# Inverse of the chunk matrix from 16x16 diagonal blocks, substituted from the last column on, with one link of 64x64 products

## The reference

```python
h = layernorm(x) * (1 + ca) + sa
x = x + ga * attn(h)
h = layernorm(x) * (1 + cb) + sb
x = x + gb * ffn(h)          # silu(w1 h) * (w2 h), gelu(h1 .), gelu(h2 .), w3 .
```

```python
A0 = -where(strict, einsum('bnid,bnjd->bnij', wk, wk) * L, 0)
A = inv(eye - A0)            # 64 x 64, unit lower triangular
v_new = A @ v - (A @ wk) @ S
```

## Time and profile before

| | us |
|---|---|
| median of 3 runs | 1741.5 (1741.11 to 1744.32) |
| the profiled execution | 1740.7 |
| its span in the trace | 1738.9 |
| PE busy | 1709.6 (98%) |
| DVE busy | 1115.6 (64%) |
| ACT busy | 965.3 (56%) |
| POOL busy | 593.6 (34%) |
| mean granted clock of TensorE | 0.991 |

### The profile page before, as it was taken

The page is one execution under the profiler, slowest core; times in us unless marked ns, Lnnn a source line. Parts: engine busy times, 40 slices in busy tenths (PEclk is TensorE's granted clock), DMA queues, the critical chain, the costliest instruction groups (busy, mean ns, idle before and its releaser), DMA issues.

```text
span 1738.9 us, 60528 instructions
## 1 busy us (share of the span) xinstructions
PE 1709.6 (98%) x25488; PEld 1644.4 (95%) x25488; DVE 1115.6 (64%) x3041; ACT 965.3 (56%) x2249; POOL 593.6 (34%) x694
## 2 busy tenths in 40 slices
PE   8799999999999999999999999999999999999999
PEld 5699999999999999999999999999999999999998
DVE  5777666666676666676666676666666666666432
ACT  4664555555555555555555555555555555565554
POOL 3544333243333243333243333243333243243111
PEclk8799999999999999999999999999999999999999
DMA  8201000000000000000000000000000000000000
GB/s 284 76 14 33 12 23 23 18 20 14 22 23 24 19 19 14 21 23 24 17 21 16 19 23 24 17 20 19 16 23 23 19 19 20 15 23 17 8 3 12
DMA packets 37356, 47.08 MB, mean 27 GB/s; under 512 B 9236, under 2 KB 29336, under 8 KB 37080
## 3 DMA queue, kind: packets, MB, share of 16 engines
q1 hardware_dynamic: 35088, 40.75, 8.5%
q10 hardware_dynamic: 1992, 2.38, 0.5%
HBM read 22.53 MB, written 8.39 MB: 18 GB/s over the span
## 4 chain that ended last, share of the span: by engine, by line
PE 93%; DVE 2%; issue 1%; POOL 1%; ACT 0%; DVEq 0%; POOLq 0%
PE mlp L1147 64%; PE mlp L1219 6%; PE solo L1147 3%; PE duo L1415 3%; PE solo L1288 3%; PE solo L1120 2%; PE duo L1336 1%; PE duo L1113 1%; PE duo L1404 1%; PE duo L1108 1%; PE duo L1309 1%; PE solo L1424 1%; PE solo L1130 1%; PE duo L1406 1%; PE duo L1300 1%
## 5 line engine op out<-in xcount | busy, mean ns | idle before, releaser
L1147 PE MATMUL mlp<-act_hi,w_hi 128*128 128x256 f32 x4096 | 967.7, 282 | 1.1 <-POOL act_lo L652 0.6
L1147 PE MATMUL mlp<-act_lo,w_hi 128*128 128x256 f32 x4096 | 945.1, 277 | 0.2
L1147 PEld LDWEIGHTS mlp<-act_hi,w_hi 128*128 128x128 f32 x4096 | 769.8, 188 | 10.1 <-POOL act_lo L652 1.3
L1147 PEld LDWEIGHTS mlp<-act_lo,w_hi 128*128 128x128 f32 x4096 | 770.1, 188 | 1.5 <-issue 0.6
L789 ACT ACTIVATE full<-mlp,scale_sb 128x256 f32<-128x256 f32 x512 | 246.2, 481 | 553.6 <-PE mlp L1147 553.4
L879 DVE TENSOR_TENSOR act_lo<-full,act_hi 128x256 fp32r<-128x256 f32 x512 | 240.2, 469 | 322.6 <-ACT act_hi L790 320.5
L652 POOL TENSOR_TENSOR act_lo<-full,act_hi 128x256 fp32r<-128x256 f32 x256 | 186.6, 734 | 496.0 <-ACT act_hi L779 496.0
L790 ACT ACTIVATE act_hi<-mlp,scale_sb 128x256 fp32r<-128x256 f32 x512 | 243.4, 475 | 0.0
L1147 PE MATMUL mlp<-xh,w_hi 128*128 128x256 f32 x768 | 186.4, 283 | 3.0 <-issue 2.4
L1147 PE MATMUL mlp<-xl,w_hi 128*128 128x256 f32 x768 | 185.4, 281 | 0.0
L591 POOL TENSOR_TENSOR rstd<-ve,minus_half 128x2 f32<-128x2 f32 x64 | 49.0, 766 | 334.2 <-DVE ve L828 334.0
(11 more groups left out here) (179 smaller groups left out, 2675.8 us busy)
## 6 DMA issues: line engine op xcount, KB each, us to landing
w_raw<-in_wts SPq DMA_DIRECT2D x22, 512.0 KB, 5.1
kg<-r SPq DMA_DIRECT2D x64, 126.0 KB
xin<-in_x SPq DMA_DIRECT2D x62, 128.0 KB
out_y<-y SPq DMA_DIRECT2D x62, 128.0 KB, 2.5
step_and_inv<-square_t SPq DMA_DIRECT2D x56, 64.0 KB, 2.0
wmod_sb<-in_wmod ACTq DMA_DIRECT2D x1, 1024.0 KB, 9.5
kg<-last SPq DMA_DIRECT2D x64, 2.0 KB
last<-r SPq DMA_DIRECT2D x64, 2.0 KB, 1.7
```

Source lines behind the costliest of these rows:

```text
L1147: mm = pe.matmul(dst, *general_ops, start=is_first and i == 0, stop=is_last and i == 1)
```

## The change

`SB` becomes 16: the diagonal blocks that VectorE inverts are 16x16, two in each half. The substitution runs from the last column (15) to column 1, and a column works on j of 16 entries, so its tiles shrink from 120 to 8 elements. The rows that it needs are rows of `low`, so the shuffles of a part stand ahead of its products. The fifteen columns are dealt to six parts (`FS_ROWS`). What is left is one link: `first_term` gives the step, VectorE subtracts it from the unit (`one_less`), ScalarE widens it to a block diagonal 64x64 table (`step_wide`), and `inverse_turned` multiplies that with the transposed inverse, whose result goes to `diag`. `lead` keeps `own`, `old_state` and `inner`; `join` becomes `solve` 1; `square_and_term`, the third link, `first_part` and `move_inverse` go. The lists are laid out anew:

```diff
-SB = 8
+SB = 16
 FS = SB - 1
+FS_ROWS = {1: (15, 14), 2: (13, 12), 3: (11, 10), 4: (9, 8), 5: (7, 6, 5), 6: (4, 3, 2, 1)}
...
-        ("l3", 6): [("ln2", 1, 0), ("expand", 0, 1)],
+        ("l3", 6): [("ln2", 1, 0), ("fs", 4, 1)],
...
-        ("l2", 0): [("old", 0, 0), ("norm", 0, 2)],
-        ("l2", 1): [("keys", 0, 0)],
-        ("l2", 2): [("join", 0, 0), ("square", 0, 2)],
-        ("l2", 3): [("length", 0, 2)],
-        ("l2", 4): [("n", 3, 1), ("state", 0, 0)],
+        ("l2", 0): [("old", 0, 0), ("norm", 0, 2), ("fs", 5, 1)],
+        ("l2", 1): [("keys", 0, 0), ("fs", 6, 1)],
+        ("l2", 2): [("solve", 1, 0), ("square", 0, 2)],
+        ("l2", 3): [("length", 0, 2), ("expand", 0, 1)],
+        ("l2", 4): [("state", 0, 0), ("n", 1, 1), ("step", 0, 1)],
         ("l2", 5): [("unit", 0, 2)],
-        ("l2", 6): [("attn_out", 0, 0), ("residual", 0, 2)],
+        ("l2", 6): [("attn_out", 0, 0), ("n", 2, 1), ("diag", 0, 1), ("residual", 0, 2)],
...
-        ("l2", 1): [("solve", 1, 0), ("fs", 3, 1), ("expand", 0, 1), ("stats", 0, 2)],
+        ("l2", 1): [("solve", 1, 0), ("fs", 3, 1), ("stats", 0, 2)],
...
-        ("l2", 5): [("n", 2, 1), ("unit", 0, 2)],
-        ("l2", 7): [("n", 3, 1)],
+        ("l2", 5): [("fs", 4, 1), ("unit", 0, 2), ("fs", 5, 1), ("fs", 6, 1), ("expand", 0, 1)],
+        ("l2", 6): [("n", 1, 1), ("step", 0, 1)],
+        ("l2", 7): [("n", 2, 1), ("diag", 0, 1)],
...
+            def widen(a):
+
+                act.wait_ge(step_ready, a + 1)
+                after(act, inverse_full, a)
+                for i in range(2):
+                    ins = act.activation(step_wide[:, :, HB * i:HB * (i + 1)], one_less[:], ACT.Copy, scale=con[:, CO_BLK + i:CO_BLK + i + 1])
+                ins.then_inc(wide_ready, 1)
...
+            def step_part(a):
                 dve.wait_ge(const_in, 16)
...
                 dve.wait_ge(step_full, a + 1)
...
+                dve.tensor_tensor(one_less[:], con[:, CO_UNIT:CO_UNIT + HB].unsqueeze(1).to_broadcast([P, 2 * NP, HB]),
+                                  of_head(duo[1][:, 1, 0:2 * NP * HB]), ALU.subtract).then_inc(step_ready, 1)
...
+                        for j in FS_ROWS[k]:
+                            ins = dve.stream_shuffle(rows[j], low[:, :, 0:j], [i // SB * SB + j for i in range(HB)])
+                        ins.then_inc(rows_ready, 1)
+                        dve.wait_ge(rows_ready, FS_PARTS * a + k)
+                        for j in FS_ROWS[k]:
+                            term = sub_term[:, 0:2 * NP * j].rearrange("p (m n) -> p m n", n=j)
+                            dve.wait_ge(sub_ready, SB * a + SB - j)
+                            dve.tensor_tensor(term, rows[j], sub[:, :, j:j + 1].to_broadcast([P, 2 * NP, j]), ALU.mult).then_inc(term_ready, 1)
+                            dve.wait_ge(term_ready, FS * a + SB - j)
+                            dve.tensor_tensor(sub[:, :, 0:j], sub[:, :, 0:j], term, ALU.subtract).then_inc(sub_ready, 1)
...
+            def inverse_turned(m, c):
+
+                return pe.matmul(of_head(duo[1][half(c), 1, 0:2 * NP * HB])[:, m, :], step_wide[half(c), m, :],
+                                 inv_t[half(c), m, :], start=True, stop=True)
...
-                            for c in range(2) if with_next else ():
-                                last_first = first_term(m, c, 1 - c)
```

More of the change, by code:

```diff
@@ L201, in main @@
     sub = sb("sub", [2 * NP, SB])
[L202 to L205, removed]
+    sub_rows = sb("sub_rows", [2 * NP * max(sum(rows) for rows in FS_ROWS.values())])
+    sub_term = sb("sub_term", [2 * NP * FS])
     inv = sb("inv", [2 * NP, HB])
@@ L296, in main @@
         ("check", 0), ("ready", 0), ("start", 0), ("spread", 0), ("tables", 0), ("gram", 0), ("heads", 0), ("check", 1), ("values", 0), ("gates", 0), ("warm", WARM_CHAIN),
[L297 to L298 removed]
+        ("intra", 0), *(("fs", k) for k in range(FS_PARTS + 1)), ("expand", 0), ("far", 0), ("stats", 0, 1), ("check", 2), ("n", 1),
+        ("step", 0), ("warm", WARM_LINK), ("n", 2), ("diag", 0), ("heads", 1), ("norm", 0, 1), ("round", 0), ("square", 0, 1), ("length", 0, 1),
         ("solve", 0), ("check", 3), ("unit", 0, 1), ("wr", 0), ("keys", 0), ("solve", 1), ("start", 0, 1), ("check", 4), ("round", 1), ("residual", 0), ("state", 0),
@@ L945, in part @@
                         dve.wait_ge(inv_ready, now)
-                        inv_t = square_t[:] if items is mixed else first_inv_t
-                        dve.transpose(inv_t.rearrange("p k n -> p (k n)"), inv[:].rearrange("p k n -> p (k n)")).then_inc(inv_t_ready, 1)
-                    if name == "n" and k == 1:
+                        dve.transpose(inv_t[:].rearrange("p k n -> p (k n)"), inv[:].rearrange("p k n -> p (k n)")).then_inc(inv_t_ready, 1)
+                    if name == "step":
                         step_part(a)
-                    if name == "lead" and (not isinstance(n, int) or n + 1 < STEPS):
-                        step_part(n + 1)
-                    if name == "n" and k == 2:
-                        first_part(a)
-                    if name == "join" and (not isinstance(n, int) or n + 1 < STEPS):
-                        first_part(n + 1)
                     if name == "state":
@@ L1327, in part @@
-                        for m in range(2 * NP) if k == 1 else ():
-                            for c in range(2):
-                                mm = first_term(m, c, c)
-                        for e, q, c, i in quarters if k > 1 else ():
-                            rows, m = quarter(c, i), e * NP + q
-                            if k == 2:
-                                mm = square_and_term(m, rows)
-                            if k == 3:
-                                back = quarter(1 - c if items is mixed else c, i)
-                                mm = pe.matmul(of_head(duo[1][back, 1, 0:2 * NP * HB])[:, m, :], square_t[rows, m, :], first_two[rows, m, :], start=True, stop=True)
@@ L1359, in part @@
-                    if name == "lead" or name == "solve" and k == 0:
-                        with_next = name == "lead" and (not isinstance(n, int) or n + 1 < STEPS)
-                        pe.wait_ge(const_in, 16)
-                        if with_next:
-                            pe.wait_ge(cross_ready, n + 2)
-                            pe.wait_ge(inv_ready, n + 2)
+                            pe.wait_ge(wide_ready, now)
+                        for m in range(2 * NP):
+                            for c in range(2):
+                                if k == 1:
+                                    mm = first_term(m, c)
+                                if k == 2:
+                                    mm = inverse_turned(m, c)
@@ L1365, in part @@
+                        mm.then_inc({1: step_full, 2: inverse_full}[k], 1)
+                    if name == "lead" or name == "solve" and k == 0:
+                        pe.wait_ge(const_in, 16)
                         pe.wait_ge(far_ready, now)
```

122 lines of the change are left out of this document (35 added, 87 removed), and 6 rows, old and new, of the table third.

## The result

| | before | after |
|---|---|---|
| median of 4 runs, us | 1742.0 | 1866.1 (1862.7 to 1867.6) |
| ratio, 95% interval | | 1.071 (1.069 to 1.073) |
| span of the profiled execution | 1738.9 | 1865.5 |
| mean granted clock of TensorE | 0.991 | 0.974 |

What follows compares the result with a forecast made beforehand. TensorE's full queue was taken to bound the kernel: 28 x (1.55 + 1.16) = 75.9, plus 6 for chunks 0 to 3, gave +82, 1823.5 us against 1741.5; forecast 1800 to 1850, range 1784 to 1855.

Steps and rivals of the forecast that it cites:

- TensorE's own sum, +1.55 a step: TensorE's queue in steady steps: products removed against new blocks `n` 1 and `n` 2, net +1.55 us a step.
- Riding free: In the lead, first terms interleaved with `inner` used quadrants that stood free, so taking them out saves nothing.
- The edge of 0.28: attn_out ahead of small products instead of an FFN product takes 1.82 instead of 1.54 us, 0.28 more.
- The wait, 1.16 a step: TensorE ahead of `n` 1 waits for VectorE's inverse, there at 941.79 against 940.63: 1.16 us each step.
- rival 1: VectorE keeps up, small operations at the spacing of independent ones, no wait: 1788 us; chance 0.12.
- Rival 2: Mask loads hold VectorE, or its chain is longer elsewhere: waits of 2 to 3.3 us, 1851 to 1887; chance 0.17.
- No other new wait in steady steps, ScalarE's copies free: Steady steps: only the inverse's wait is new; ScalarE's two copies to `step_wide` are wanted late and cost nothing.
- The two terms: Steady steps: TensorE's own 1.55 and the wait of 1.16 us, 28 times, 75.9 us.
- Chunks 0 to 3, +6 (0 to +14): Lists of chunks 0 to 3, ahead of the steady steps: about +6 us, between 0 and +14.
- chunk 0's longer substitution: VectorE in chunk 0: about 4 us longer, covered by its missing links and by waits for the weights.
- The half of `third` that I priced at 4: Second half of `third`: substitution parts, unit and `expand` in l2-5 take about 6.3 us; about 4 lost once.

Runs made afterwards that it cites:

- later: Changed kernel with the link of `n` 1 one column later, behind column 5 of l2 instead of column 4: 1823.1 us, ratio 1.045.
- apart: Kernel before with the lead's 16 first-term products placed behind the 16 inner products instead of between them: 1759.9 us, ratio 1.009.
- swap: Kernel with that link one column later (1823.1 us), and in steady steps `n` 2 ahead of attn_out instead of behind it: 1822.4 us.

## Why the prediction was wrong

- **TensorE's own sum, +1.55 a step**: right. `later` has it alone, 1.58; `n` 1 and `n` 2 take 1.05 each (1.01 forecast), the lead keeps its 1.0. Riding free was right too (`apart`). The edge of 0.28 is there in the blocks, but `swap` shows that it is not a price of this order.
- **The wait, 1.16 a step**: right, with rival 1 out. (51.6 - 6.17 - 3.09 - 8.93) / 27 = 1.24. VectorE's chain took 9.54 us, from 1011.29 to TensorE's start at 1020.83, where the sum had 9.35; the 21 small operations of `fs` 5 and 6 took 4.11 instead of 3.97. Rival 2's mask loads cost nothing: the shuffles of a part stand 0.09 to 0.13 apart. A dependent operation of 56 elements starts 1013.84 - 1013.59 = 0.25 behind the one before, as the earlier trace rows had it. The Trainium skill, "Vector Engine (DVE) Microarchitecture Reference", section "Measured stream behaviour on trn2", gives 75 ns and 1.04 ns a column, from which I estimate 0.13 for it, and by that there would have been no wait; the trace of the changed kernel does not agree either where an operation needs the last.
- **No other new wait in steady steps, ScalarE's copies free**: right. The two terms and their 28 steps were to give 75.9; the 27 steps have 74.0, and the 28th, which has no wait, is 2.0 longer.
- **What the wait brings with it: left out.** The step that failed is the one that priced a wait at its own length. I had read a granted clock of 1.00 as a property of the steady steps, and it no longer held where a wait and a thin link stood ahead of the FFN. Nine times the FFN behind them ran at 0.68, +1.5 each: 14.5 us in all, with one stop of 1.3 for which the profile names no releaser.
- **The place of the tiles: left out.** The change has `+ 26`, and I costed it at nothing without a word. With the block of 96 it is 13.3 us, of which about 8 are shown to come from the place.
- **Chunks 0 to 3, +6 (0 to +14): mis-sized**, 22.7. I had costed chunk 0's longer substitution as covered; its wait for the inverse is 6.17, and the end of `alone` and `second` together come 7.4 later. The half of `third` that I priced at 4 has a wait of 8.93 and a slow column of 16 products behind it (3.71 instead of 2.16), as the first half has (3.09, and 3.58 instead of 2.03). The parts' own time there was right (6.3 forecast, 9.4 from 173.91 to 183.32 with the 3 us beside GpSimd); left out were the residual and the statistics ahead of them, and GpSimd beside them. The rows of the changed kernel for chunk 0 and for both halves of `third`:

```profile
37.57 1.92 PE L1097 MATMUL duo<-inv,cross 64*64 64x32 f32 x32 [6.17 <-DVE inv L942]
```

```profile
132.36 1.92 PE L1097 MATMUL duo<-inv,cross 64*64 64x32 f32 x32 [3.09 <-DVE inv L942]
...
183.46 1.92 PE L1097 MATMUL duo<-inv,cross 64*64 64x32 f32 x32 [8.93 <-DVE inv L942]
```

The three add up: 82 + 16.7 + 14.5 + 13.3 = 126.5, against a measured difference of the spans of 126.6. Only all three together carry the time out of the range: even without the smallest, 13.3, it would have been 1852.8, inside 1855. The sign and the mechanism of the terms that I had were right; the range was too narrow above because it held only their bounds, and none for a clock that falls or for tiles that move.

## What to carry to other kernels

A kernel whose TensorE never stands has its clock as a hidden asset: price a new wait ahead of thin products at more than its length, here some 1.24 for the wait and 0.5 more on average for the FFN behind it. Take the cheap way out first: 32x32 products instead of block diagonal 64x64 ones behind the wait took the slow stretches away with the wait still there, and the link one column later took both. And when tiles move, even by unused words, measure the padding alone before anything else is explained; here it alone cost the kernel before up to 3.2%.

## What the runs showed of the hardware

- The distance between two operands' tiles in the SBUF acts on the spacing of the FFN's products (fp32r operands, 128x256) at full granted clock; which two tiles it is was not isolated: 96 products in 10.98, 11.40 or 11.59 us, and 1740 to 1795 us for one and the same program, back after 256 bytes.
- The granted clock fell to 0.50 for a part of the FFN block (0.68 over its 5.40 us) behind 9 of 15 waits of 1.35 to 1.37 us followed by 1.05 us of products in two quadrants; with 0.67 us of products in four quadrants behind waits of 1.34 to 1.36, behind none of 12.
- Three small VectorE operations (0.23 us alone), each started just after a two-input GpSimd operation of 1.2 us, took 1.1 to 1.3 us and ended just after it.
- 16 products in two quadrants take 1.05 us, 32 of a quarter of the weights in four quadrants 0.67; of two blocks of 16 in different quadrants, the second costs 0.72 queued behind the first, and nothing interleaved with it.
